# The down-projection weight staging loop of an attention and gated-MLP kernel: its DMAs issued from ScalarE instead of GpSimd

## Chip, cores and metric

One Trainium2 chip, eight cores, one program on all of them. Each core works on half of the 2048 rows of one of the four batch entries (two cores share an entry) and no core waits for another. The metric is the device time in microseconds of the slowest of the eight cores. A core has TensorE (PE), VectorE (DVE), ScalarE (ACT), GpSimd (POOL) and SyncE (SP), each with its own in-order stream of instructions, and 16 DMA engines that carry the transfers issued from any of them.

## What is computed

```python
def reference(x, w_atten, w_proj, w_gate, w_up, w_down):
    xn = _layernorm(x, axis=-1)
    s = attn(xn, w_atten, w_proj)     # qkv, RoPE, causal softmax over 16 heads of 128, projection
    h = silu(xn @ w_gate) * (xn @ w_up)
    h_sparse = keep_2_largest_of_4(h)
    g = _silu(h_sparse @ w_down)      # w_down: 8192 x 2048
    return x + s * g
```

x is 4 x 2048 x 2048, in float32; the matrix products run on bf16 operands.

## The kernel before

The program is written as one Python pass that appends to a list per engine (class KB). `kb.emit` appends an instruction with the semaphore values that it waits for; `kb.dma` (line 65) appends a DMA start to the list of the engine that it names first, so the DMA waits its turn there. Every DMA carries line 66 in the profile. The order of the lists is the order of execution.

The phases, in order of time in the profiled execution:

1. Layer norm of the whole batch entry (to 185 us): x is loaded in four parts, normalized and kept in SBUF as bf16 (`xn`).
2. Attention (185 to 2304 us): a loop over `NG` = 8 groups of two heads (`for g in range(NG)`, from line 320). A group has first a **staging part**, then the K, Q and V projections, then the attention blocks of the two heads.
3. The output projection (2304 to 2509 us), from `d_y`, the attention output in DRAM, to `d_s`.
4. Gate and up projections with the 2-of-4 selection (2509 to 3663 us), whose weights `wgu` come in 128 loads of 1 MB from SyncE (`wgu_load`, 128 x 16 x 128 float32, pieces of 512 bytes in DRAM).
5. The down projection and the final sum (3663 us to the end). Its weights are read from `d_wdb`, a bf16 copy of `wd` in DRAM.

The staging part of phase 2 is what makes `d_wdb`. It has eight rounds per group (`for j in range(8)`, 64 rounds in all). A round loads 1 MB of `wd` (float32, 128 partitions x 16 pieces of 512 bytes) into the one buffer `wdp_st`, VectorE casts it to bf16 into the one buffer `wdp_bf` (line 331), and a DMA of 512 KB writes that to `d_wdb` (called the spill here). Load s waits for cast s-1, cast s waits for load s and for spill s-1, spill s waits for cast s. Load and spill are both in POOL's list. POOL's list has in phase 2 only these and the four writes of `d_y` per group, which stand behind the group's eight rounds.

On VectorE's list the eight casts of a group stand ahead of the three casts of the group's K, V and Q weights (line 346), and the first projection on TensorE (line 366) waits for the K cast. The K, V and Q weights are loaded by SyncE (2 MB each, pieces of 1 KB) into two buffers `wstag2`; those of K and V are issued during the group before, that of Q after the K cast. ScalarE evicts the projections (lines 379, 429), computes the exponentials (line 471), and ends each attention block with the copy of line 508, after which VectorE writes `y_sb` (line 511) and POOL stores it to `d_y`.

Of the kernel before, what the change touches and what calls it, by code (L numbers as in the profile page):

```python
# [114 lines left out]
def build_nc():  # L115
# [19 lines left out]
    d_wdb = nc.dram_tensor("d_wdb", [128, NIC * C], BF16).ap()  # L135
# [30 lines left out]
    kb = KB(nc)  # L166
# [133 lines left out]
    wdp_st = A.alloc(16 * 128)  # L300
# [21 lines left out]
    for g in range(NG):  # L322
        for j in range(8):
            s_ = g * 8 + j
            fcw, qi = s_ // 4, s_ % 4
            srcw = wd[qi * 2048:(qi + 1) * 2048, fcw * 128:(fcw + 1) * 128]\
                .rearrange("(c p) d -> p c d", p=128)
            t_wpl = kb.dma("gpsimd", wdp_st[:].rearrange("p (c d) -> p c d", d=128),
                           srcw, "dWQ0" if s_ % 2 == 0 else "dWQ1",
                           [wdp_cast.get(s_ - 1)] + (xn_done if s_ == 0 else []))  # L330
            t_wpc = E("vector", lambda e: e.tensor_copy(wdp_bf[:], wdp_st[:]),  # L331
                      [t_wpl, wdp_spill.get(s_ - 1)], "DVE")
            wdp_cast[s_] = t_wpc
            t_wps = kb.dma("gpsimd", d_wdb[:, s_ * 2048:(s_ + 1) * 2048],
                           wdp_bf[:], "dWDS0" if s_ % 2 == 0 else "dWDS1", [t_wpc])
            wdp_spill[s_] = t_wps
        toks_w = {}
# [592 lines left out]
```

How the kernel before makes its waits and increments, by code:

```python
                def body(handle):  # L76
                    for waits, fn, inc in ops:
                        for s, v in waits:
                            handle.wait_ge(sems[s], v)
                        ins = fn(handle)
                        if inc is not None:
                            s, by = inc
                            ins.then_inc(sems[s], by)
```

## Time and profile before

| | |
|---|---|
| median of 2 runs | 4179.31 us (4172.73 to 4185.9) |
| the profiled execution | 4201.99 us |
| its span, slowest core (core 6) | 4200.5 us |
| spans of the other cores | 4120.2 to 4191.1 us |
| busy share | PE 67%, PEld 29%, DVE 32%, ACT 14%, POOL 7% |
| phase 2, staging parts | 8 stretches of some 80 to 95 us in which PE does nothing |

The span is the time from the first to the last instruction of a core; the 1.5 us between it and the execution's time lie around it. The profile lists each engine's busy time, who waited for whom, the chain of work that ended last, and the packets of the DMA engines. Queue names with a q (SPq, POOLq) are the DMA-issuing instructions of an engine; their length is the time of issue and not that of the transfer, which is given as "us to landing".

### The profile page before, as it was taken

How to read it: one execution, taken by the hardware profiler on the slowest of the kernel's cores; microseconds unless marked ns; L12 is line 12 of the kernel's file. 1: busy time of each engine (PE TensorE's matmuls, PEld its weight loads, DVE VectorE, ACT ScalarE, POOL GpSimd, SP SyncE). 2: the span in 40 equal slices, each digit the busy share in tenths (PEclk: the TensorE clock that was granted, in tenths of full speed). 3: DMA queues.
4: the chain of work that ended last, by engine and by line, in shares of the span. 5: the costliest groups of instructions: out<-in, count | busy, mean ns of one | idle time of the engine just before them, and what ended most of it. 6: DMA issues, size and time to landing. Idle time of an engine off the chain costs nothing.

```text
span 4200.5 us, 34928 instructions; the slowest of 8 cores (4120.2 to 4200.5 us)
## 1 busy us (share of the span) xinstructions
PE 2803.4 (67%) x12592; PEld 1202.0 (29%) x12592; DVE 1328.4 (32%) x2087; ACT 603.5 (14%) x1102; POOL 308.5 (7%) x420
## 2 busy tenths in 40 slices
PE   2238276282762826628377567888899888679698
PEld 0014041140411404114041223333344433334244
DVE  4521131221312213122131104665656666501010
ACT  1102112021120211302112011111111111100000
POOL 0010100101001010010100010000101000101010
PEclk7569687696876968859688898999999999889899
DMA  4350320503305023050220617655465656265664
GB/s 152 103 157 3 99 84 20 165 3 88 96 15 170 3 79 104 15 170 3 82 62 15 221 64 178 147 125 135 109 152 137 151 120 157 56 227 196 215 208 160
DMA packets 398793, 466.99 MB, mean 111 GB/s; under 512 B 10144, under 2 KB 337824, under 8 KB 394144
## 3 DMA queue, kind: packets, MB, share of 16 engines
q1 hardware_dynamic: 354080, 309.54, 25.8%
q0 software_dynamic: 44544, 155.22, 12.7%
q8 instruction: 104, 1.70, 0.2%
q14 instruction: 65, 0.53, 0.1%
HBM read 393.41 MB, written 71.30 MB: 111 GB/s over the span
## 4 chain that ended last, share of the span: by engine, by line
PE 51%; DMA 23%; DVE 14%; issue 7%; ACT 2%; SPq 1%; POOL 1%; DVEq 0%; ACTq 0%; POOLq 0%
DMA arena<-wd 13%; PE ps L721 12%; PE ps L808 11%; PE ps L366 6%; PE ps L420 5%; PE ps L467 4%; DMA d_hT<-arena 3%; PE ps L484 3%; PE ps L490 3%; PE ps L455 3%; DVE arena L502 3%; DMA arena<-wqT 2%; DMA d_s<-arena 2%; DVE arena L331 2%; PE ps L563 2%
## 5 line engine op out<-in xcount | busy, mean ns | idle before, releaser
L721 PE MATMUL ps<-arena 128*128 128x512 bf16 x4096 | 955.4, 392 | 33.1 <-DVE arena L697 33.0
L366 PE MATMUL ps<-arena 128*128 128x512 bf16 x1536 | 365.2, 393 | 748.5 <-DVE arena L346 748.5
L721 PEld LDWEIGHTS ps<-arena 128*128 128x128 bf16 x4096 | 410.1, 101 | 523.9 <-issue 84.8
L808 PE MATMUL ps<-arena 128*128 128x512 bf16 x2048 | 454.6, 384 | 77.0 <-DMA arena<-d_wdb 77.0
L366 PEld LDWEIGHTS ps<-arena 128*128 128x128 bf16 x1536 | 152.5, 100 | 954.0 <-issue 784.4
L502 DVE RECIPROCAL arena<-ps 1x512 f32<-1x512 f32 x32 | 107.1, 3346 | 762.6 <-PE ps L484 762.6
L808 PEld LDWEIGHTS ps<-arena 128*128 128x128 bf16 x2048 | 206.0, 101 | 325.3 <-issue 83.8
L471 ACT ACTIVATE arena<-ps 128x512 bf16<-128x512 f32 x384 | 229.3, 597 | 322.0 <-PE ps L467 317.7
L331 DVE CAST arena<-arena 128x2048 bf16<-128x2048 f32 x64 | 78.6, 1227 | 620.5 <-DMA arena<-wd 620.5
L420 PE MATMUL ps<-arena 128*128 128x256 bf16 x2048 | 230.8, 274 | 0.0
L379 ACT CAST arena<-ps 128x512 bf16<-128x512 f32 x96 | 56.2, 585 | 1074.7 <-PE ps L366 1043.4
L420 PEld LDWEIGHTS ps<-arena 128*128 128x128 bf16 x2048 | 201.8, 99 | 28.5
L733 DVE TENSOR_TENSOR arena<-arena,ps 128x256 f32<-128x256 f32 x256 | 105.4, 417 | 303.4 <-ACT arena L730 302.9
L730 ACT ACTIVATE arena<-ps 128x256 f32<-128x256 f32 x256 | 98.1, 383 | 703.0 <-PE ps L721 643.7
L697 DVE CAST arena<-arena 128x2048 bf16<-128x2048 f32 x128 | 157.0, 1226 | 132.7 <-DMA d_s<-arena 90.7
L467 PE MATMUL ps<-arena 128*128 128x512 bf16 x384 | 159.8, 416 | 57.8 <-PE ps L455 2.0
L563 PE MATMUL ps<-arena 128*128 128x512 bf16 x512 | 124.9, 399 | 83.7 <-ACT arena L570 47.8
L66 POOL DMA_DIRECT2D d_hT<-arena x128 | 97.2, 759 | 1053.7 <-DVE arena L733 785.0
L831 DVE TENSOR_TENSOR arena<-arena 128x512 f32<-128x512 f32 x32 | 22.2, 693 | 481.1 <-ACT arena L819 481.1
L455 PE MATMUL ps<-arena 128*128 128x512 bf16 x384 | 168.0, 437 | 4.9 <-ACT arena L429 4.9
L490 PE MATMUL ps<-arena 128*128 128x512 bf16 x384 | 159.3, 415 | 0.0
L484 PE MATMUL ps<-arena 128*1 128x512 bf16 x384 | 154.1, 401 | 7.5 <-ACT arena L471 6.7
(72 smaller groups left out, 1821.5 us busy)
## 6 DMA issues: line engine op xcount, KB each, us to landing
arena<-wgu SPq DMA_DIRECT2D x128, 1024.0 KB, 14.2
arena<-wd POOLq DMA_DIRECT2D x64, 1024.0 KB, 8.0
arena<-d_wdb SPq DMA_DIRECT2D x32, 2048.0 KB, 8.0
d_wdb<-arena POOLq DMA_DIRECT2D x64, 512.0 KB, 3.0
arena<-xT SPq DMA_DIRECT2D x4, 4096.0 KB, 15.0
arena<-wkT SPq DMA_DIRECT2D x8, 2048.0 KB, 14.6
arena<-wvT SPq DMA_DIRECT2D x8, 2048.0 KB, 9.4
arena<-wqT SPq DMA_DIRECT2D x8, 2048.0 KB, 10.6
```

Of the source, the lines that this page charges most:

```text
L331: t_wpc = E("vector", lambda e: e.tensor_copy(wdp_bf[:], wdp_st[:]), [t_wpl, wdp_spill.get(s_ - 1)], "DVE")
L366: tok = E("tensor", lambda e, f=f, h2=h2, bank=bank, tile=tile, wv_=wv_: e.matmul(ps[bank][:], wv_[:, f, h2 * 128:(h2 + 1) * 128], xnv[:, ...
L420: tok = E("tensor", lambda e, f=f, tc=tc, bank=bank: e.matmul(ps[bank][:, 0:256], xnv[:, f, tc * 128:(tc + 1) * 128], wvv[:, f, :], start= ...
L455: t_s = E("tensor", lambda e, qpos=qpos, h2=h2, a=a, sbank=sbank: e.matmul(ps[[0, 1, 4][sbank]][:], kh[:, h2 * T + qpos * 128:h2 * T + (qp ...
L467: t_mm = E("tensor", lambda e, mi=mi, sbank=sbank: e.matmul(ps[[0, 1, 4][sbank]][:], id_sb[:], mk_sb[:, mi * 512:(mi + 1) * 512], start=Fa ...
L471: t_e = E("scalar", lambda e, sbank=sbank, slot=slot: e.activation(pT[slot][:], ps[[0, 1, 4][sbank]][:], AF.Exp, bias=EXP_BIAS, scale=EXP_ ...
L484: last=(qi == nL - 1): e.matmul(ps[3][0:1, :], ones_colb[:, 0:1], pT[slot][:], start=first, stop=last),
L490: first=(qi == 0), last=(qi == nL - 1): e.matmul(ps[2][:], vg[:, qpos * 256 + h2 * 128:qpos * 256 + (h2 + 1) * 128], pT[slot][:], start=fi ...
L502: t_rcp = E("vector", lambda e: e.reciprocal(recip[0:1, :], ps[3][0:1, :]), [den_last, prev_rpe], "DVE")
L563: wpv=wpv: e.matmul(ps[bank][:], wpv[:, yc, cc * 128:(cc + 1) * 128], yav[:, yc, tt2 * 512:(tt2 + 1) * 512], start=(yc == 0), stop=(yc == ...
L721: tok = E("tensor", lambda e, f=f, tc=tc, bank=bank, gv=gv: e.matmul(ps[bank][:], xnv[:, f, tc * 128:(tc + 1) * 128], gv[:, f, :], start=( ...
L808: tok = E("tensor", lambda e, ic=ic, bank=bank, wdv=wdv: e.matmul(ps[bank][:], wdv[:, ic, :], hTv[:, ic, :], start=(ic == 0), stop=(ic == ...
```

## The change

The first argument of two `kb.dma` calls goes from "gpsimd" to "scalar". Buffers, semaphores, waits and sizes stay.

```diff
-            t_wpl = kb.dma("gpsimd", wdp_st[:].rearrange("p (c d) -> p c d", d=128),
+            t_wpl = kb.dma("scalar", wdp_st[:].rearrange("p (c d) -> p c d", d=128),
                            srcw, "dWQ0" if s_ % 2 == 0 else "dWQ1",
                            [wdp_cast.get(s_ - 1)] + (xn_done if s_ == 0 else []))
             t_wpc = E("vector", lambda e: e.tensor_copy(wdp_bf[:], wdp_st[:]),
                       [t_wpl, wdp_spill.get(s_ - 1)], "DVE")
             wdp_cast[s_] = t_wpc
-            t_wps = kb.dma("gpsimd", d_wdb[:, s_ * 2048:(s_ + 1) * 2048],
+            t_wps = kb.dma("scalar", d_wdb[:, s_ * 2048:(s_ + 1) * 2048],
                            wdp_bf[:], "dWDS0" if s_ % 2 == 0 else "dWDS1", [t_wpc])
```

On POOL, from the last round of group 0 into group 1, before the change (`arena<-wd` is the load, `d_wdb<-arena` the spill):

```order
L66 DMA arena<-wd 128x16x128
L66 DMA d_wdb<-arena 128x2048 [waits DVE]
L66 DMA d_y<-arena 128x512 [waits DVE] x4
L66 DMA arena<-wd 128x16x128
L66 DMA d_wdb<-arena 128x2048 [waits DVE]
```

And the same engine in the changed kernel, from its start:

```order
L66 DMA d_y<-arena 128x512 [waits DVE] x32
L66 DMA d_s<-arena 128x512 [waits ACT] x32
L66 DMA d_hT<-arena 128x4x128 [waits DVE] x2
```

The 64 loads and 64 spills are gone from POOL; its first DMA is now the first write of `d_y`.

On ACT, across the same boundary of two groups, before the change:

```order
L471 ACTIVATE arena<-ps 128x512 [waits PE] x16
L508 COPY arena<-ps 128x512 [waits PE,DVE]
L379 CAST arena<-ps 128x512 [waits PE] x2
L379 CAST arena<-ps 128x512 [waits PE,DVE] x10
L429 CAST arena<-ps 128x256 [waits PE,DVE]
```

In the changed kernel the group boundary on ACT begins:

```order
L471 ACTIVATE arena<-ps 128x512 [waits PE] x16
L508 COPY arena<-ps 128x512 [waits PE,DVE]
L66 DMA arena<-wd 128x16x128
L66 DMA d_wdb<-arena 128x2048 [waits DVE]
L66 DMA arena<-wd 128x16x128
L66 DMA d_wdb<-arena 128x2048 [waits DVE]
```

and, after eight such pairs, ends:

```order
L66 DMA arena<-wd 128x16x128
L66 DMA d_wdb<-arena 128x2048 [waits DVE]
L379 CAST arena<-ps 128x512 [waits PE] x2
L379 CAST arena<-ps 128x512 [waits PE,DVE] x10
L429 CAST arena<-ps 128x256 [waits PE,DVE]
```

A group's sixteen DMAs now stand between the last copy of the group before and the group's first eviction of a projection. The lists of PE, DVE and SP are the same in both kernels.

## Rows read from the trace of the kernel before

**Rows 1.** Waits of core 6: who waited for what, us in total, times, longest.
```profile
PE ps L366 <- DVE arena L346: 748.5, 8, 112.9
DVE arena L331 <- DMA arena<-wd: 620.5, 64, 16.3
DVE arena L346 <- DMA arena<-wqT: 67.9, 8, 11.1
```

**Rows 2.** Timeline, start of group 1: start, length, engine, line, what [idle before].
```profile
456.90 0.59 ACT L508 COPY arena<-ps 128x512 f32<-128x512 f32 x1 [6.31 <-PE ps L505]
...
458.96 0.54 POOL L66 DMA_DIRECT2D d_y<-arena  x1 [29.42 <-DVE arena L511]
459.49 1.17 POOL L66 DMA_DIRECT2D arena<-wd  x1
467.50 1.23 DVE L331 CAST arena<-arena 128x2048 bf16<-128x2048 f32 x1 [9.08 <-DMA arena<-wd]
469.26 0.55 POOL L66 DMA_DIRECT2D d_wdb<-arena  x1 [8.60 <-DVE arena L331]
469.80 1.17 POOL L66 DMA_DIRECT2D arena<-wd  x1
477.52 1.23 DVE L331 CAST arena<-arena 128x2048 bf16<-128x2048 f32 x1 [8.79 <-DMA arena<-wd]
```

**Rows 3.** Timeline, end of the staging part of group 1.
```profile
541.75 4.50 DVE L346 CAST arena<-arena 128x4096 bf16<-128x4096 f32 x2
542.39 1.77 POOL L66 DMA_DIRECT2D d_wdb<-arena  x1 [11.09 <-DVE arena L331]
544.12 0.37 SPq L66 DMA_DIRECT2D arena<-wqT  x1
544.29 9.34 PE L366 MATMUL ps<-arena 128*128 128x512 bf16 x32 [87.54 <-DVE arena L346]
550.27 0.58 ACT L379 CAST arena<-ps 128x512 bf16<-128x512 f32 x1 [92.78 <-PE ps L366]
```

**Rows 4.** Timeline, end of the layer norm: ACT waiting for DVE.
```profile
162.92 0.68 DVE L251 TENSOR_TENSOR arena<-arena 1x512 f32<-1x512 f32 x1
...
163.70 0.63 ACT L253 ACTIVATE arena<-arena 1x512 f32<-1x512 f32 x1 [5.46 <-DVE arena L251]
```

**Rows 5.** All 64 loads of wd, the line on the landings.
```profile
DMA to landing us min/median/max: 7.2/8.0/15.5
```

**Rows 6.** All loads of wgu: issue in ns (min/median/max), and the landings.
```profile
L66 SPq DMA_DIRECT2D arena<-wgu x128: 367/3860/11628, 2509.3 to 3552.5; - x128
...
DMA to landing us min/median/max: 7.1/14.2/24.4
```

**Rows 7.** DMA issues of 2613.5 to 2614.5 and of 2893 to 2894 us.
```profile
arena<-wgu SPq DMA_DIRECT2D x1, 1024.0 KB, 7.3
...
arena<-wgu SPq DMA_DIRECT2D x1, 1024.0 KB, 9.7
```

**Rows 8.** DMA rates (40 slices) and issues, 469 to 473 and 3268 to 3271 us.
```profile
GB/s 0 0 0 0 0 0 0 0 0 0 0 0 0 246 328 369 369 492 451 328 451 451 369 369 369 492 164 0 0 0 164 164 164 246 82 205 82 205 0 246
...
arena<-wd POOLq DMA_DIRECT2D x1, 1024.0 KB, 7.6
...
3268.65 9.41 SPq L66 DMA_DIRECT2D arena<-wgu  x3
...
GB/s 0 0 0 0 0 0 0 0 0 0 0 0 0 0 0 0 0 0 0 0 0 0 20 48 82 68 61 82 68 61 48 82 41 55 61 55 82 61 75 96
```

**Rows 9.** Queues of 483 to 486 and of 2616 to 2620 us: packets, MB, share of 16 engines.
```profile
q0 software_dynamic: 216, 0.87, 97.2%
...
q1 hardware_dynamic: 2128, 1.08, 102.3%
```

**Rows 10.** DMA issues of 185 to 200 us, the start of group 0.
```profile
arena<-wvT SPq DMA_DIRECT2D x1, 2048.0 KB, 28.7
arena<-wd POOLq DMA_DIRECT2D x1, 1024.0 KB, 15.5
```

## The prediction

> **What bounds the kernel now.** I read the waits first. TensorE waits 748.5 us for the K cast, in eight waits, one per group, and VectorE, on whose list that cast stands, waits 620.5 us in 64 waits for the loads of wd [rows 1]. So the staging part is a chain with nothing beside it: load, cast, spill issue, next load issue, and only then the projections. The timeline of group 1 shows the links [rows 2]. Cast 467.50 to 468.73; spill issued at 469.26, that is 0.53 us later; load issued at 469.80, 0.54 us after that; next cast at 477.52, 7.72 us after the issue. One round is 10.02 us. Whatever shortens a link shortens the program 64 times, for no other engine has work in that stretch: PE's 87.54 us of idle time end when the K cast is done [rows 3]. Over all rounds the wait is 620.5 / 64 = 9.70 us; less the 0.53 and the 0.54 this leaves 8.63 us from load issue to cast, and 8.51 to landing, since in the round shown the load lands 7.6 us after 469.80, at 477.40, and 0.12 us pass before the cast [rows 2, 8]. The median landing is 8.0; the longest, 15.5, pulls the mean up [rows 5].
>
> **The change, part by part.** Bytes, waits and buffers stay. What changes is who issues, and which kind of queue carries the transfers: those of POOL appear as q0, those of SP as q1, and q1 cuts them differently [rows 9]. ScalarE issues no DMA in this trace, so I price it by SP, the other engine with such a queue, and keep POOL's price as the other end.
>
> a) *Reaction to the cast.* POOL starts 0.53 us after the cast's end [rows 2]. ACT starts 163.70 after a DVE instruction that ended at 162.92 + 0.68 = 163.60, so 0.10 us [rows 4]; SP starts its load of wqT at 544.12, within 0.1 us of the end of the first of the two casts begun at 541.75 [rows 3]. Gain 0.43 x 64 = 27.5 us. Ends: 0 and 27.5. I take 27.5, since it is ACT's own row.
>
> b) *Issue of the spill, ahead of the next load.* 0.54 us on POOL [rows 2], 0.37 on SP [rows 3]. 0.17 x 56 = 10 us (the last spill of a group has no load behind it). Ends: +10, and -35 if ACT took 0.6 us longer, for which no row speaks. I take 10.
>
> c) *The load itself.* The nearest rows are the wgu loads, which have the same shape and come by SP: shortest 7.1, median 14.2, but most of them queue behind each other, and an issue that takes 3.86 us shows that [rows 6]. Two that found their queue idle landed after 7.3 and 9.7 us [rows 7], and even these had more loads issued right behind them. The quiet ends are therefore 7.1 against 7.2: nearly equal. Two things cancel. Data starts later on POOL's queue: load issued at 469.80, its first bytes at 472.0, so 2.2 us [rows 2, 8]; on SP's queue issue at 3268.65, first bytes at 3269.65, so 1.0 us [rows 8]. But SP's queue builds up slowly, 60 to 80 GB/s for over a microsecond, as if one DMA engine after the other got its share. And its packets are small: 97.2% x 16 x 3 us / 216 = 216 ns per 4 KB on q0, 102.3% x 16 x 4 us / 2128 = 31 ns per 512 bytes on q1, so 246 ns per 4 KB, 30 ns more, or 256 x 30 / 16 = 0.5 us per load [rows 9]. The spill ahead of the load costs nothing new: it holds the engines from 470.3 to 471.7, 1.4 us [rows 8], and the last engines of a slow build-up start after that. I take a gain of 0.2 us per load, 13 us. Ends: 7.2 us in every round, gain 1.31 x 64 = 84; 9.7 us in every round, loss 1.19 x 64 = 76.
>
> The Trainium skill ("DMA: Bandwidth & Descriptors", section "Why small descriptors are slow (HBM only)") speaks against this step: a fixed cost of about three cycles per packet inside the DMA engine. The extra 30 ns for seven more packets per 4 KB agree with it. The same page ("Latency and other measured facts") puts the first byte at about 600 ns for the hardware path and 1 us for GpSimd's; the rows show 1.0 and 2.2 us, a larger difference, and the rows decide.
>
> d) *Start of a group.* On POOL the first load stands behind the write of d_y, which waits for line 511: issue at 459.49. On ACT it stands behind the copy that ends at 457.49, and waits for nothing else that is late, so it starts at about 457.6 [rows 2]. Gain 1.9 x 7 = 13.5 us. The d_y write moves under the load.
>
> e) *After the last round.* The last spill is issued at 542.39 and takes 1.77 us while DVE casts; the load of wqT starts beside it at 544.12 [rows 3], and DVE waits 67.9 us for wqT [rows 1]. An earlier spill is out of its way sooner. Ends 0 and 8 (a microsecond per group); I take 3.
>
> f) *Group 0.* The first load of wd runs against K's and V's 4 MB: 15.5 us, V's load 28.7 [rows 10]. Taking turns packet by packet with SP's, small packets get a smaller share. Ends: -15 and +3; I take -3.
>
> g) *What ACT now holds up.* Behind its sixteen DMAs stands the first eviction of a projection. The last spill is issued by about 542.3, the eviction comes at 550.27 [rows 3]: 7.9 us of cover. Even an issue of 3.86 us [rows 6] would fit. Cost 0. POOL has nothing left that anyone waits for.
>
> Sum: 27.5 + 10 + 13 + 13.5 + 3 - 3 = 64 us off the profiled execution, 4202 - 64 = 4138. That execution is 23 us above the median of the runs; the forecast for the median is 4179 - 64 = **4115 us**, 1.5% less. A measurement of this kernel tells about 2% (84 us) from no change.
>
> **Rivals.** All without term c, the sum is 51 us.
>
> *Loads at their shortest.* The mean of POOL's loads (8.51) is well above its shortest (7.2), from neighbours' traffic; if ACT's loads land near 7.2 nearly always, c is 84 and the time 4179 - 51 - 84 = 4044. Over 2% from a mean landing of 8.51 - (84 - 51) / 64 = 8.0 on. For it: the median of POOL's is already 8.0 and data starts 1.2 us earlier. Against: the shortest of the two kinds are equal.
>
> *Issue is not what it seems.* ACT reacts and issues as slowly as POOL: a and b vanish, 4115 + 37 = 4152. For it: no ACT DMA in the trace. The Trainium skill (same page, "Issuing engines are not separate DMA queues") says that DMAs run on the same 16 engines whoever starts them and that only a sequencer's issue time is saved; by it c would be 0. That leaves 4179 - 51 = 4128, no change that can be told.
>
> *One queue for ACT and SP.* Both kinds may be served in order of issue. Then the first load lands after V's, some 17 us later than now (28.7 - 15.5 = 13, since both are issued within a microsecond, and 4 of its own data), 2 of which come back in the next round: 4115 + 12 = 4127.
>
> *Small packets lose (slower).* If 2048 small packets per load suffer under eight cores as the wgu loads do, a load takes 9.7 to 14.2 us: 4179 - 51 + 76 = 4204 at the first, 4179 - 51 + 5.69 x 64 = 4492 at the second. It is slower than before from a mean landing of 8.51 + 51 / 64 = 9.3 on and by over 2% from 8.51 + (84 + 51) / 64 = 10.6 on. For it: the medians of rows 6 and 7. Against: in staging one load is in flight at a time, and VectorE, TensorE and SP are quiet.
>
> **How the numbers follow.** Forecast, with its own range 4096 to 4150: 0.46. Loads at their shortest, 4040 to 4095: 0.33. Slow issue on ACT: 0.10. One queue: 0.04. Small packets lose: 0.07. Faster by over 2% is the second case, 0.33; slower by over 2% the last, 0.07; the rest, 0.60, is within 2%. The range 4050 to 4190 leaves out the far ends of c on both sides.
>
> **What would show it.** The spill should start 0.1 us after the cast, the load about 0.4 us after the spill, the first load of a group 0.1 us after line 508. VectorE's wait for wd should be near 620 - 64 + 3 = 560 us (all terms but e), and PE's wait at line 366 near 748 - 61 = 688. Packets of q0 fall by 64 x 384, and q1 gains 64 x 2048 small ones. It is wrong if the median landing of wd is under 7.6 or over 8.8, if ACT's issues take over 1 us each, or if the first eviction of a group is late.

## The result, and the profile after

| | before | changed |
|---|---|---|
| median of all executions | 4200.7 us (10) | 4121.6 us (11) |
| median of those that the ratio uses | 4199.7 us (9) | 4100.8 us (8) |
| ratio | | 0.979, 95% interval 0.975 to 0.984 |
| profiled execution | 4201.99 us | 4134.25 us |
| mean span of the eight cores | 4153 us | 4060 us |

The forecast was 4115 us, 1.5% less; measured is 2.1% less, and the interval reaches to both sides of the 2% bound. The ratio, and every time given for an experiment below, leaves out executions in which one die ran at a lower clock. Kernels without a ratio have too few executions for one (the small spills and the 2 KB pieces were run once or twice, for their traces), and of them landings, rounds and waits are compared.

The waits of the changed kernel on its slowest core, now core 5, to be read beside [rows 1]:

```profile
PE ps L366 <- DVE arena L346: 653.5, 8, 106.7
DVE arena L331 <- DMA arena<-wd: 525.3, 64, 20.0
DVE arena L346 <- DMA arena<-wqT: 62.2, 8, 8.9
```

The chain is still the same and TensorE still waits for all of it, only for less. The slowest core is another one, so I compare means over the eight cores: the wait for wd falls from 601 to 500 us, TensorE's wait at line 366 from 729 to 628.

The timeline at the start of group 1 (core 5), to be read beside [rows 2]:

```profile
443.97 0.59 ACT L508 COPY arena<-ps 128x512 f32<-128x512 f32 x1 [5.54 <-PE ps L505]
443.98 0.39 ACTq L66 DMA_DIRECT2D arena<-wd  x1
...
444.79 0.69 DVE L511 TENSOR_TENSOR arena<-ps,arena 128x512 bf16<-128x512 f32 x1 [2.39 <-ACT arena L508]
446.02 0.54 POOL L66 DMA_DIRECT2D d_y<-arena  x1 [27.79 <-DVE arena L511]
450.43 1.23 DVE L331 CAST arena<-arena 128x2048 bf16<-128x2048 f32 x1 [4.95 <-DMA arena<-wd]
451.74 0.34 ACTq L66 DMA_DIRECT2D d_wdb<-arena  x1
452.11 0.46 ACTq L66 DMA_DIRECT2D arena<-wd  x1
459.63 1.23 DVE L331 CAST arena<-arena 128x2048 bf16<-128x2048 f32 x1 [7.97 <-DMA arena<-wd]
```

The round from cast to cast is 9.20 us where it was 10.02. The spill starts 0.08 us after the cast's end, the load 0.37 us after the spill. The first load of the group is issued as the copy of line 508 starts, not when it ends.

The end of the staging part of group 1, beside [rows 3]:

```profile
515.49 4.49 DVE L346 CAST arena<-arena 128x4096 bf16<-128x4096 f32 x2
515.65 0.33 ACTq L66 DMA_DIRECT2D d_wdb<-arena  x1
517.85 0.37 SPq L66 DMA_DIRECT2D arena<-wqT  x1
518.02 8.94 PE L366 MATMUL ps<-arena 128*128 128x512 bf16 x32 [74.20 <-DVE arena L346]
...
523.60 0.59 ACT L379 CAST arena<-ps 128x512 bf16<-128x512 f32 x1 [79.04 <-PE ps L366]
```

ScalarE is through with its DMAs at 515.98 and its first eviction is due at 523.60: nothing is held up. The spill's issue took 1.77 us on POOL while VectorE cast, and takes 0.33 us here beside the same casts. The Trainium skill ("DMA: Bandwidth & Descriptors", section "SWDGE vs HWDGE vs iDMA") says that POOL writes its descriptors where VectorE's fast modes can lock it out, and that ScalarE's queue never touches that path. The trace agrees in so far as POOL's issue is the longer one beside the casts (1.77 us, and 0.54 away from them [rows 2]) and ScalarE's is not; the lock itself no row shows.

DMA queues of the whole execution, and the landing times of all loads of wd on core 5 [beside rows 5]:

```profile
q1 hardware_dynamic: 354080, 309.54, 27.4%
q10 hardware_dynamic: 141312, 100.67, 8.8%
q0 software_dynamic: 17920, 54.54, 4.0%
...
DMA to landing us min/median/max: 6.0/7.4/19.8
```

ScalarE's transfers have a queue of their own, q10, apart from SP's q1. The load is now 2048 packets of 512 bytes where it was 256 of 4 KB, and lands sooner all the same. That is the surprise, and the experiments are about it.

Not all of the gain reaches the end. The SP timelines (first issue of a phase) of before and of the changed kernel, each on its slowest core:

```profile
2509.30 1046.82 SPq L66 DMA_DIRECT2D arena<-wgu  x128
3663.02 10.36 SPq L66 DMA_DIRECT2D arena<-d_hT  x2
```

```profile
2403.96 1083.09 SPq L66 DMA_DIRECT2D arena<-wgu  x128
3592.96 11.08 SPq L66 DMA_DIRECT2D arena<-d_hT  x2
```

The gate and up phase begins 105 us earlier and ends 70 us earlier. Over the eight cores its mean length went from 1134 to 1150 us.

### The profile page after: what moved, and what is told of

It is laid out like the page before. It is cut to its first block, busy times and chain, and to the rows that moved or that the text cites. A ratio compares the mean times of both kernels' runs of the same rounds, so it can differ in the third digit from the quotient of the medians.

```text
span 4132.7 us, 34928 instructions; the slowest of 8 cores (3992.8 to 4132.7 us)
## 1 busy us (share of the span) xinstructions
PE 2807.4 (68%) x12592; PEld 1204.8 (29%) x12592; DVE 1329.0 (32%) x2087; ACT 603.3 (15%) x1102; POOL 189.2 (5%) x292
## 4 chain that ended last, share of the span: by engine, by line
PE 47%; DMA 26%; DVE 14%; issue 6%; SPq 4%; ACT 2%; ACTq 1%; DVEq 0%; POOLq 0%
DMA arena<-wd 12%; PE ps L808 11%; PE ps L366 7%; PE ps L721 6%; PE ps L420 6%; DMA arena<-wgu 5%; DMA d_hT<-arena 5%; SPq L66 4%; PE ps L467 4%; PE ps L484 3%; PE ps L490 3%; PE ps L455 3%; DVE arena L502 3%; PE ps L563 2%; DVE arena L331 2%
## 5 line engine op out<-in xcount | busy, mean ns | idle before, releaser
L420 PEld LDWEIGHTS ps<-arena 128*128 128x128 bf16 x2048 | 203.9, 100 | 27.5
L662 PE MATMUL ps<-arena 128*128 128x128 bf16 x512 | 52.5, 228 | 172.2 <-DVE arena L645 169.2
```

Of the source, the lines that this page charges most:

```text
L420: tok = E("tensor", lambda e, f=f, tc=tc, bank=bank: e.matmul(ps[bank][:, 0:256], xnv[:, f, tc * 128:(tc + 1) * 128], wvv[:, f, :], start= ...
```

## The experiments

The two theories named A and B are each run's own. "Landing" is the time from issue of a load of wd to its landing; the medians of this table are over eight cores and seven groups (group 0, with its own traffic, left out), "first" is the first load of a group, which has no spill ahead of it, "others" the seven after it. The round is the mean from load issue to load issue, group 0 included. Time is the ratio to the kernel before, where there is one.

| kernel | first | others | round | time |
|---|---|---|---|---|
| before: load and spill on POOL | 7.7 | 7.5 to 7.9 | 10.6 | 1 |
| changed: both on ScalarE | 6.1 | 7.0 to 7.2 | 9.2 | 0.979 |
| load ScalarE, spill POOL | 6.1 | 8.0 to 8.1 | 9.8 | 0.993 |
| load POOL, spill ScalarE | 7.6 | 7.2 to 8.1 | 10.0 | 0.993 |
| both ScalarE, load first | 6.1 | 6.4 to 7.0 | 8.5 | 0.966 |
| both POOL, load first | 7.5 | 8.9 to 9.1 | 11.0 | |
| changed, small spill | 6.1 | 6.2 | 8.5 | |
| before, small spill | 7.5 | 7.5 to 7.8 | 10.3 | |
| changed, 2 KB pieces | 5.2 | 5.8 to 5.9 | 8.1 | |
| before, 2 KB pieces | 5.6 | 6.3 to 6.8 | 9.3 | |

### One of the two moved: `e1_load_act`, `e2_spill_act`

```diff
# e1_load_act: t_wpl only
-            t_wpl = kb.dma("gpsimd", ...
+            t_wpl = kb.dma("scalar", ...
# e2_spill_act: t_wps only
-            t_wps = kb.dma("gpsimd", ...
+            t_wps = kb.dma("scalar", ...
```

> Only the load of wd is issued from ScalarE, the spill stays on POOL. Theory A (a load lands as soon as its own queue starts and what stands ahead of it in that queue is done): the load is issued 0.1 us after the cast, has no spill ahead in its queue, and lands after 6.1 to 7.0 us; one round (load issue to load issue) 7.6 to 8.6 us against 9.2 with both on ScalarE and 10.6 before; ratio to before about 0.96, faster than with both moved. Theory B (the kind of queue does not matter, only ScalarE's quicker reaction and the shorter issue are gained): landing stays near 8 us, round 9.4 us, ratio 0.98.

Measured: ratio 0.993 (0.989 to 0.997), round 9.8. A missed: the load lands after 8 us, later than with both moved. B's landing came, though its round (9.4) and its ratio (0.98) did not. A lone load (the first of a group) does land after 6.1 us. The timeline of core 4 shows what meets the others:

```profile
457.14 1.23 DVE L331 CAST arena<-arena 128x2048 bf16<-128x2048 f32 x1 [8.21 <-DMA arena<-wd]
458.45 20.41 ACTq L66 DMA_DIRECT2D arena<-wd  x3
458.91 0.54 POOL L66 DMA_DIRECT2D d_wdb<-arena  x1 [8.90 <-DVE arena L331]
```

The load is issued at 458.45, the spill at 458.91 from POOL. The queues of 458.4 to 463 and of 463 to 466 us on this core (q10 is the load, q0 the spill):

```profile
q10 hardware_dynamic: 1160, 0.59, 63.8%
...
q10 hardware_dynamic: 904, 0.45, 50.5%
q0 software_dynamic: 144, 0.52, 42.8%
```

The spill's packets come only in the second half of the load's, over 4 us after the spill's own issue, and the load ends almost 2 us later than a lone one. By time, moving the load alone gave a third of the gain.

> Only the spill is issued from ScalarE, the load stays on POOL. Theory A: the load still starts its data 2.2 us after issue and lands after a median of 7.6 us; only the 0.54 us for the spill's issue ahead of it go, round 10.0 us, no gain at the start of a group; ratio about 0.99. Theory B (it is the writing of the bf16 copy that profits from the other queue, and the load only lands earlier because of it): the landing falls to 7.2 us or less and the ratio nears the 0.98 of the full change.

Measured: ratio 0.993 (0.988 to 0.998), round 10.0, landing unchanged. A held in each number. A spill in another queue costs nothing here: it is issued 0.5 us before the load, and POOL's load starts its data 2.0 us after its issue (median of the packets), when the spill is done.

By time the two halves give 0.7% each and the whole 2.1%. In the staging parts, though, the halves add up: TensorE's wait at line 366, as a mean over eight cores, is 729 us before, 663 with the load moved, 694 with the spill moved and 628 with both, so 66 + 35 = 101 against 100. Having both in one queue gives nothing extra there. Part of what is missing in the time of `e1_load_act` lies where its code is that of the kernel before: its gate and up phase was 1167 us long in the trace, against 1134. Why is open (see `e11_after_again`).

### Load ahead of the spill: `e3_load_first_act`, `e4_load_first_pool`

```diff
-    wdp_bf = A.alloc(16 * 64, BF16)
+    wdp_bf2 = [A.alloc(16 * 64, BF16) for _ in range(2)]
...
             wdp_cast[s_] = t_wpc
+            if j < 7:
+                wdp_load(s_ + 1)
             t_wps = kb.dma(...)
```

`wdp_load(s)` issues the load of round s; the first load of a group is issued ahead of its first cast, as before.

> Both on ScalarE, but load s+1 is issued ahead of spill s, with a second bf16 buffer so that the cast waits for the spill before last. Theory A (on ScalarE's queue the spill ahead costs the load a full microsecond): the load lands after 6.1 us in every round as the first of a group does now, round 7.6 us, ratio about 0.955. Theory B (the engines are shared, so the spill costs the same wherever it stands): landing 7.1 us, round 8.5 us, ratio 0.968.

Measured: ratio 0.966 (0.959 to 0.972), landing 6.4 to 7.0, round 8.5. Between the two: the load is quicker than behind the spill, but not as quick as alone, since the packets of the spill issued 0.4 us after it come 4.5 to 7 us after the load's issue, before the load is done. By time B's figure came, by landing neither.

> The same order as in the run before, but both on POOL. Theory A (POOL's queue starts so late that the spill ahead is already done): the landing does not change (median 7.7 us), only the 0.54 us of the spill's issue go, round 9.9 to 10.0 us, ratio 0.99. Theory B (order is what counts and the queue is not): the landing falls by a microsecond here too, round 9.0 us, ratio 0.975.

Both theories missed. The landing rises to 9 us and the round to 11.0, and the rounds are longer on all cores. One execution of six can be compared: 4230 us, above the 4164 to 4218 of the kernel before on the same chip. Two rows of its trace (core 4):

```profile
478.21 1.16 POOL L66 DMA_DIRECT2D arena<-wd  x1 [10.01 <-DVE arena L338]
479.36 0.57 POOL L66 DMA_DIRECT2D d_wdb<-arena  x1
```

The spill is issued right behind, and the load lands 1.4 us later than the first of a group (8.9 against 7.5), about the 1.4 us for which a spill holds the engines [rows 8]. What was hidden in the kernel before, when the spill went ahead and was done before the load's first bytes, is now in the open.

### The spill's share measured: `e5_small_spill_act`, `e6_small_spill_pool`

```diff
-            ... d_wdb[:, s_ * 2048:(s_ + 1) * 2048], wdp_bf[:], ...
+            ... d_wdb[:, s_ * 256:(s_ + 1) * 256], wdp_bf[:, 0:256], ...
-                              d_wdb[:, fc * 4 * 2048:(fc + 1) * 4 * 2048],
+                              d_wdb[:, fc % 2 * 8192:(fc % 2 + 1) * 8192],
```

> The changed kernel with spills of 64 KB in place of 512 KB (the down projection then reads these few columns again and again, so the output is not the reference's). Theory A (a load's landing is start-up plus its own data plus whatever part of the spill's 1.3 us falls after the start-up): on ScalarE's queue, which starts after 1 us, the median landing falls from 7.1 to 6.1 to 6.3 us in all rounds. Theory B (the first load of a group lands after 6.1 us for another reason, the pause before it): it stays at 7 us.

> The kernel before with the same small spills. Theory A: POOL's queue starts a load 2.2 us after issue, when the full spill is already done, so the median landing stays at 7.5 to 7.7 us. Theory B (a spill costs the load behind it about a microsecond on any queue): it falls to 6.7 us.

Measured on ScalarE: 6.2 us in every round with a spill ahead, where it was 7.1. On POOL: 7.5 to 7.8, as before. The same lines of the two traces, on their slowest cores:

```profile
L66 ACTq DMA_DIRECT2D arena<-wd x64: 385/457/464, 183.7 to 1963.7; - x64
...
DMA to landing us min/median/max: 5.9/6.2/20.7
```

```profile
L66 POOL DMA_DIRECT2D arena<-wd x64: 1166/1171/1302, 185.5 to 2084.2; - x64
...
DMA to landing us min/median/max: 7.4/7.8/15.4
```

A holds on both: a spill ahead costs the load a microsecond on the queue that starts early, and nothing on the one that starts late. The DMA rates of the changed kernel show it (core 5, 40 slices of 0.1 us; a lone load issued at 443.98, and a spill at 460.93 with a load at 461.30 behind it):

```profile
GB/s 0 0 0 0 0 0 0 0 0 0 0 0 0 0 0 0 0 0 0 0 77 143 215 179 179 174 138 108 56 108 148 210 230 236 287 230 246 282 266 297
```

```profile
GB/s 0 0 0 0 0 0 0 0 0 0 0 0 287 287 573 246 451 573 123 573 41 164 410 82 123 205 246 205 164 312 118 113 128 205 220 307 323 312 292 292
```

The windows begin at 443 and 460.5. The lone load's first bytes come at 445.0, 1.0 us after issue. In the second row the spill runs from 461.7. Where the load begins behind it, the size of the packets tells, since the spill's have 4 KB and the load's 512 bytes; the packets of 461.6 to 463.4 and of 463.4 to 464.4 us:

```profile
DMA packets 116, 0.48 MB, mean 264 GB/s; under 512 B 0, under 2 KB 0, under 8 KB 116
...
DMA packets 387, 0.23 MB, mean 233 GB/s; under 512 B 16, under 2 KB 375, under 8 KB 387
```

The load's first packet comes at 463.46, 2.2 us after its issue, when the spill is nearly over. So in the rounds with a spill ahead ScalarE's load starts its data no earlier than POOL's: 2.25 and 2.24 us after issue, as medians of 392 loads on eight cores each (1.06 for ScalarE's lone loads, 1.12 behind a small spill). It still lands 0.6 us sooner (7.1 against 7.7), and that is gained between the first bytes and the landing: 4.8 us against 5.4. Why this stretch is shorter, with eight times as many packets, no run separates.

### The packets: `e7_2k_pieces_act`, `e8_2k_pieces_pool`

```diff
-            srcw = wd[qi * 2048:(qi + 1) * 2048, fcw * 128:(fcw + 1) * 128]\
-                .rearrange("(c p) d -> p c d", p=128)
+            srcw = wd[s_ % 16 * 512:(s_ % 16 + 1) * 512, s_ // 16 * 512:(s_ // 16 + 1) * 512]\
+                .rearrange("(c p) d -> p c d", p=128)
...
-            ... wdp_st[:].rearrange("p (c d) -> p c d", d=128), ...
+            ... wdp_st[:].rearrange("p (c d) -> p c d", d=512), ...
```

> The changed kernel with loads of the same size cut as 4 pieces of 2 KB per partition in place of 16 of 512 bytes (other columns of wd, so the output is not the reference's). Theory A (start-up rules, small packets cost 0.5 us per load): median landing 6.5 us. The rival that small packets cost nothing or even help: 7.1 us as now. A landing under 6.0 would mean that the number of packets is the main cost.

> The kernel before with the same 2 KB pieces. Theory A: POOL's queue packs the 512-byte pieces into 4 KB packets already, so little changes, median landing 7.3 to 7.7 us and still a microsecond above ScalarE's. Rival (the size of the pieces in DRAM is what differs in cost): both kernels gain alike.

Measured: 5.8 us on ScalarE. A's 6.5 was too high, and 5.8 is under the 6.0 that was to mean that the number of packets is the main cost: the mean of all loads falls by 1.2 us (7.42 to 6.23), where I had worked out 0.5. On POOL it is 6.3 to 6.8 us, where A had said that nothing would change; its mean falls by 1.3 us (8.09 to 6.82), so the rival, that both kernels gain alike, is what came. POOL pays for pieces before the first byte too: its issue is shorter.

```profile
L66 POOL DMA_DIRECT2D arena<-wd x64: 756/761/892, 184.2 to 2039.0; - x64
...
DMA to landing us min/median/max: 5.5/6.8/15.7
```

0.76 us against 1.17 in [rows 2]. With this earlier start (a first load's data 1.5 us after issue) the spill ahead begins to cost on POOL as well: first load 5.6, others 6.3 to 6.8. So on both queues a landing is start-up, plus the part of a spill ahead that outlasts the start-up, plus data. Alone, the two queues are now 0.4 us apart (5.6 against 5.2) and not 1.6: most of POOL's lag hangs on the number of pieces.

### Out of the chain: `e9_spread_pool`, `e10_spread_act`, `e12_spread_pool_again`

```diff
+    wdp_load(0)
     for g in range(NG):
-        for j in range(8):
-            ... load, cast, spill
...
                 emit_rope(*pend)
+            if ui == 6:
+                wdp_rounds(1)
...
         emit_rope(*pend)
+        wdp_rounds(3)
...
                 y_spills.append(t_ysp)
+                wdp_rounds((2, 1, 1, 0)[2 * h2 + a])
```

`wdp_rounds(n)` emits n times the cast of the load in flight, its spill, and the next load. In `e10_spread_act` the two DMAs inside it are issued from ScalarE.

> Both DMAs on POOL as before, but the eight rounds of a group are spread over its work: one cast after the seventh projection, three after the last, and 2, 1, 1, 0 after the attention blocks, each next load issued right after the cast, so that loads run while TensorE works. Theory A (the chain costs time only because nothing stands beside it): the 689 us of staging go, less some 6 us per group for the K and V casts and a few us of DVE work in the way; ratio to before 0.84 to 0.86. Theory B (the transfers or the casts then collide with the projections, or TensorE's clock is granted less when it no longer pauses, and most of it comes back): ratio over 0.90.

> The same spread order, with both DMAs issued from ScalarE. Theory A (ScalarE pays for waiting in order once it has work): each spill waits on ScalarE's list for a load and a cast with the evictions of V and the exponentials behind it, some 25 us after the projections and 10 us in the first long block of every group, so 200 to 300 us of the gain are lost; ratio 0.90 to 0.92, slower than with POOL. Theory B (the quicker queue wins here too): ratio at or below that of the run with POOL.

> The spread order with both DMAs on POOL once more, for its ratio to the kernel before with an interval: theory A 0.84 to 0.86 again; theory B, if the first figure was one lucky chip, over 0.87.

Measured: 3504 and 3513 us on the first chip; on the second a median of 3492 us (four executions) and a ratio of 0.835 (0.829 to 0.841) to the kernel before, 0.853 to the changed one by the quotient 0.835 / 0.979. The waits of that run on its slowest core (line 374 is the old 366, 335 the cast, 354 the casts of K, V and Q):

```profile
DVE arena L335 <- DMA arena<-wd: 218.4, 24, 11.0
...
PE ps L374 <- DVE arena L354: 69.4, 8, 40.6
```

TensorE's wait is 69.4 us in place of 748.5 [rows 1], 40.6 of it the very first. VectorE still waits for wd, but only in 24 of 64 rounds, and the profile names no engine but POOL, for its spills, as waiting for these casts. The loads land hardly sooner than before (medians of 7.4 to 7.8 us, by POOL). TensorE's mean granted clock is 0.91 where it was 0.84. Before, it was 0.50, the lower of its two levels, from 460 to 500 and from 500 to 540 us, where TensorE stood in a staging part, and 1.00 from 550 to 600, where it worked; without these pauses the mean of the attention phase is 0.90 in place of 0.77. B's fear was without ground.

From ScalarE the spread order takes 3822 us (median of four), on the same chip as the 3504 and 3513 us from POOL and the 4124 us of the changed kernel. That is 0.93 of the latter and 0.91 of the kernel before (4182 and 4225 us there). Its waits (line 440 evicts V, 482 is the exponential, 431 V's matmul, 495 a matmul that needs the exponentials):

```profile
ACT arena L440 <- DVE arena L335: 197.2, 8, 25.7
...
PE ps L431 <- ACT arena L440: 166.1, 8, 21.9
ACT arena L482 <- DVE arena L335: 138.1, 21, 12.8
...
PE ps L495 <- ACT arena L482: 130.8, 56, 11.8
```

A holds, with the 25 us after the projections as expected: ScalarE stands at a spill that waits for a cast, and V's eviction and the exponentials stand behind it. TensorE waits 166 + 131 = 297 us behind them, where from POOL the same two waits are 0 and 7 us; that is 290 us of the 313 between the two times, somewhat more than the 200 to 300 that A had allowed.

### The changed kernel again: `e11_after_again`

> The changed kernel once more, for its ratio on this chip and a second trace: median landing of wd 7.1 us in the rounds with a spill ahead and 6.1 us in the first of a group, staging 600 to 615 us of a core's span against 689 before, ratio 0.975 to 0.985. If the gate and up phase is again 16 us longer than before, the change gives that back; if it is not, that is scatter from one execution to the next.

Measured: median 4124 us, on another chip than the 4101 us above, and 0.98 of the two executions of the kernel before that can be compared there (4182 and 4225 us; no interval). Landing 6.1 and 7.1 to 7.3; staging 606 us. The gate and up phase was 1152 us long, again longer than 1134. But in the other kernels, whose code is the same there, it was between 1113 (e5) and 1167 (e1), and one and the same kernel had 1132 (e9) and 1118 (e12). That is no pattern of who issues in staging, and e5 with both on ScalarE has the shortest. Why the changed kernel had 1150 twice stays open.

## Why the prediction was right, and where its steps were off

The chain and what bounds it were as read, and the time and its direction came out within the stated range. How close the figure came is in part luck. The terms of the gain add up to 107 us and not 64, while the kernel before measured 4201 us and not the 4179 that the forecast started from. Put on 4179 us, the measured ratio of 0.979 gives 4093 us: in the range of the rival "loads at their shortest" (4040 to 4095) and not in the forecast's own (4096 to 4150). The prediction's own sign of being wrong, a median landing under 7.6 us, came too: the medians of the eight cores are 6.8 to 7.4. VectorE's wait for wd and TensorE's wait at line 366 fell by 101 and 100 us, where it had 60 and 61.

The terms, from the traces, as means over eight cores:

| term | forecast | measured |
|---|---|---|
| a, reaction to the cast | 27.5 | 29 (landing to spill issue 1.93, now 1.48; x 64) |
| b, issue of the spill | 10 | 10 (0.54, now 0.36; x 56) |
| c and f, the load | 13 - 3 | 43 (mean landing 8.09, now 7.42; x 64) |
| d, start of a group | 13.5 | about 17.5 (2.5 x 7) |
| e, wqT | 3 | about 8 (mean landing 10.40, now 9.36; x 8) |
| sum | 64 | 107 |

Staging (from a group's first load issue to the K cast) went from 689 to 607 us and the rest of the attention phase from 1403 to 1383, together 102 us of these 107; 93 of them are left in the mean span.

*Term c was mis-sized*, 0.2 us per load where 0.67 was measured. The step that failed is "the quiet ends are therefore 7.1 against 7.2: nearly equal". The 7.1 came from wgu loads that have others issued right behind them, and I had noted that; a lone load of this shape lands after 6.1 us, which the first loads of the groups and e5 show. The second half of the step, that the spill ahead costs nothing new on a quick queue, was wrong as well: it costs 0.9 to 1.0 us (e5 against the changed kernel). The two errors pulled in opposite directions, and what was left is 0.67 us per load. The first bytes, 1.0 us after issue against 2.2, were read rightly, but the whole 1.2 us is there only for a load with nothing ahead of it, 8 of 64; behind a spill ScalarE's load starts its data after 2.2 us as well (e5's section), and lands sooner by what comes after.

The slow build-up that was to cancel the earlier start wasn't there either. The 60 to 80 GB/s came from a wgu load with others issued around it. The lone load on ScalarE moved 138 GB/s in its first microsecond of data and 243 in the next, by the row shown with e5. POOL's load of [rows 2, 8] moved 156 and 234, in its window of 472 to 476 us:

```profile
GB/s 164 164 164 246 82 205 82 205 0 246 82 164 164 287 123 246 246 287 410 328 246 410 410 369 328 205 410 287 328 328 287 369 246 328 328 287 205 369 246 123
```

The rival "loads at their shortest" had 33 in 100 and asked for a mean landing under 8.0, counted from the 8.51 of core 6. Less 0.67 that is 7.8, so it is this rival that came nearest, though not with landings at their shortest throughout. (The 8.51 was worked out from the waits; core 6's landings themselves have a mean of 8.40.)

*Term d.* The issue does not wait for the end of the copy ahead of it on ScalarE: 443.98 against 443.97 for its start. That is 0.6 us more per group. (1.9 x 7 is 13.3, not 13.5.)

*Term f.* The first load of group 0 lands after 17.6 us (mean), 13.7 before, and the second after 8.4, 9.7 before: a loss of 2.5, forecast 3. "One queue for ACT and SP" falls with q10.

*Terms a, b and g* came as worked out. "Issue is not what it seems" falls: ScalarE issues the load in 0.46 us and the spill in 0.33. The Trainium skill's rule that only a sequencer's issue time is saved ("DMA: Bandwidth & Descriptors", section "Issuing engines are not separate DMA queues") is too narrow here: of 107 us, 43 are earlier landings. What the same section says of transfers of all queues interleaving on the same 16 engines fits e1, where a spill in another queue makes the load land 1.9 us later.

*Small packets.* They did not turn the result, yet they are dear: 2 KB pieces take 1.2 us off the mean landing on ScalarE and 1.3 on POOL (e7, e8).

## What to carry to other kernels

In a chain of one load, one cast and one store, price the queue by a load that is alone in it, and the store by where its packets fall: issued ahead of a late-starting load it was free, from the same queue or another (e6, e2), and issued behind the load it was not, from the same queue or another (e4, e1). But look first at who waits for the chain: a quicker queue made it 12% shorter (689 to 607 us) and the kernel 2% faster, and putting the same rounds beside the matmuls took 16.5% off the kernel's time. There the quick queue was the wrong one, because its engine had work to do behind the waits.

## What the runs showed that I had not expected

- POOL's queue carries the 512-byte pieces of a load in 4 KB packets and ScalarE's in 512-byte packets, and the latter lands some 1.5 us sooner when alone (6.1 against 7.5 to 7.7).
- A spill issued half a microsecond behind a load disturbs it more from another queue than from the load's own: landing 8.0 (e1) against 6.4 to 7.0 (e3).
- With the load first, the spill's issue on ScalarE takes a median of 1.85 us over eight cores (nine in ten between 1.2 and 3.4), not 0.33. Two rows of e3 (core 7):

```profile
464.97 0.37 ACTq L66 DMA_DIRECT2D arena<-wd  x1
465.37 1.66 ACTq L66 DMA_DIRECT2D d_wdb<-arena  x1
```
